# A three-layer interaction network with a row tower: layer 1's operand is written without its norm by ScalarE, and the norm is applied in two VectorE steps where layer 1 ends

## The chip, the cores and the metric

One core of a Trainium2 chip. The metric is the device time of one launch in microseconds (us). PE is TensorE, DVE is VectorE, ACT is ScalarE, POOL is GpSimd, SP is SyncE (it issues most transfers). Float32 throughout.

## The reference

For each of 512 samples, 39 fields pick one row of 16 numbers each from their tables; this is x (39 fields by 16 dimensions d). Three layers follow, each with 128 units:

```
prev = x                                     # 39 x 16, later 128 x 16
for k in 0, 1, 2:
    t[o, d] = sum over m, h of  W_k[m, h, o] * x[m, d] * prev[h, d]   + b_k[o]
    t = t / sqrt(sum over o and d of t*t)    # one norm per sample
    logit_k = t ; prev = t
z = sum over d of the three t's, concatenated        # 384 per sample
y = relu(relu([z, dense] @ W_top1 + b_top1) @ W_top2 + b_top2) @ W_top3
```

The norm is one number per sample. Layer 1 is linear in prev, so a norm left out of prev can be applied to layer 1's sum before the bias.

## The kernel before, in words

**Tiles.** 512 samples are 16 tiles of 32; a tile has 32 x 16 = 512 columns (sample, d), one PSUM bank wide. Units lie on the 128 partitions. Tiles 1 to 14 run in a hardware loop (`Fori`) on each engine, tiles 0 and 15 are written out before and behind it, with hand-written order in each and semaphores between them.

**A layer (k = 1 or 2) of a tile** is 11 chunks c0 to c10 of `xb`, the rows of x broadcast over the partitions by DMA. DVE writes the products z = `t_ps[k-1]` x `xb` (L651), PE multiplies them with the weights. Chunks c0, c2, c7, c10 are direct (2 or 3 fields, L820). The other seven hold four fields that are treated as two pairs in a scheme like Strassen's: POOL makes the sums `t2` (L354) and `t41` (L357) of the products (for c5 and c6 of layer 1 DVE and ACT make `t2`, L664 and L517), and PE takes 28 matmuls on products and sums (L834), the last ones after a wait on `t41`. z is a ring of 14 rows, so DVE waits for PE to free rows. Layer 0 works on `xr`, products of x with shifted x (L634), into `acc0` (L811).

**Order on PE** in a tile: layer 1 (c0 to c10), layer 0 of the next tile, layer 2 (c0 to c5), the small matmuls for the norms (`add_partitions`, L879), layer 2 (c6 to c10).

**Where layer 1 ends.** After c9 ACT copies parts of the pair sums (`carry`, L527 to L531), DVE adds them in five small steps into `v` (`shared_sums`, L672 to L683), then `add_shared` (L685): for k = 1 one scalar_tensor_tensor, raw12 = acc1 + bias + v (L691). ACT copies raw12 to `t_ps[1]` (L538), layer 2's operand, and squares it (L541). For k = 2 `add_shared` is already two steps: acc2 += v (L694), raw12 = acc2 x norm of layer 1 (L697), and ACT adds the bias (L546, L547).

**Where layer 0 ends.** ACT reads `acc0` twice: squares (L494) and the value with its bias into `traw0` (L495). DVE sums both over d (`norm_sums`, at c5 of layer 2). At c8 DVE makes 1/norm of all three layers (`normalize`), at c9 it writes the features and then `t_ps[0]` = (acc0 + bias) x norm (`scale0`, L741), layer 1's operand for the next tile. PE's next layer 0 waits for `traw0` and `scale0`.

**POOL** also issues the gathers of table rows (L317): ten per tile, seven of them after c9 of layer 1, one after c6 and two after c9 of layer 2, for the tile after next. Before tile 0 it issues the gathers of tiles 0 and 1. **SP** writes gathered rows to DRAM (`write_rows`, L290) and loads `xb` (L410), x (L277) and `xr` (L283). At the start its order is: `xr` of tile 0; wait until all of it has landed; `xb` c0 to c5; the rows of tile 1 (a wait for their gathers); `xb` c6 to c10; x and `xr` of tile 1.

**Before tile 0** PE does layer 0, then the norm's matmul; DVE runs sum_squares, sum_d, normalize, features and scale0 before its first product of layer 1.

Of the kernel before, what the change touches and what calls it, by code (L numbers as in the profile page):

```python
# [5 lines left out]
ALU = mybir.AluOpType  # L6
# [5 lines left out]
P = 128  # L12
# [7 lines left out]
N = TILE_B * EMB  # L20
# [111 lines left out]
def build(nc, ids_in, base_in, masks_in, table, xt, xq, dense_t, w0a, w0b, w1, w2, b0, b1, b2,  # L132
          wt1, bt1, wt2, bt2, wt3, out):
    ctx = ExitStack()
    with ctx:
# [25 lines left out]
        ones = sb("ones", [P, UNITS // 2])  # L161
        traw0 = sb("traw0", [P, N])
        raw12 = sb("raw12", [P, N])
# [20 lines left out]
        h1, h2 = z[:, 0:4, :], z[:, 4:6, :]  # L184
        y_sb = traw0[:, 0:P]

# [38 lines left out]
        v_step, v_used = sem("v_step"), sem("v_used")  # L225
        scaled_ready = sem("scaled_ready")
        t1_ready, t0_ready = sem("t1_ready"), sem("t0_ready")
        sq_ready = [sem(f"sq_ready{k}") for k in range(LAYERS)]
        raw_ready = [sem("raw_ready0"), None, sem("raw_ready2")]
        ssum_ready = [sem(f"ssum_ready{k}") for k in range(LAYERS)]  # L230
# [70 lines left out]
        def _(pool):  # L301
# [71 lines left out]
            gather(0, range(GROUPS))  # L373
            mix_rows(0)
            gather(1, range(GROUPS))
            tile(0)
# [6 lines left out]
        def _(sp):  # L383
# [81 lines left out]
            for j in range(TOP1 // P):  # L465
# [7 lines left out]
            sp.dma_start(out.rearrange("(g n) a -> g (n a)", n=P),  # L473
                         traw0[0:P:Y_AT, 0:P]).then_inc(y_written, 16)
            sp.wait_ge(y_written, 16)

        @block.scalar
        def _(act):
# [10 lines left out]
            def evacuate0(i):  # L489
                act.wait_ge(acc0_ready, i + 1)  # L490
                if not at_first(i):
                    act.wait_ge(t0_ready, i)
                    act.wait_ge(feat_ready, i)
                nc.scalar.activation(sq[:, 0, :], acc0[:, :], ACT.Square, bias=bias[:, 0:1]).then_inc(sq_ready[0], 1)  # L494
                nc.scalar.activation(traw0[:, :], acc0[:, :], ACT.Identity,  # L495
                                     bias=bias[:, 0:1]).then_inc(raw_ready[0], 1)

# [35 lines left out]
            def evacuate1(i, last=False):  # L533
                act.wait_ge(v_used, mix_no(i, 1) + 1)
                if not last:

                    act.wait_ge(z0_ready, len(LOADS0) * (i + 2))
                nc.scalar.copy(t_ps[1][:, :], raw12[:, :]).then_inc(t1_ready, 1)  # L538
                if not at_first(i):
                    act.wait_ge(ssum_ready[2], i)  # L540
                nc.scalar.activation(sq[:, 1, :], raw12[:, :], ACT.Square).then_inc(sq_ready[1], 1)  # L541

# [55 lines left out]
        def _(dve):  # L598
# [86 lines left out]
            def add_shared(i, k):  # L685
                n = mix_no(i, k)
                dve.wait_ge(z_used, chunks_to(i, k, NCH - 1))
                dve.wait_ge(v_step, 5 * n + 5)
                dve.wait_ge(p1_ready, n + 1)
                if k == 1:  # L690
                    nc.vector.scalar_tensor_tensor(raw12[:, :], acc[1][:, :], bias[:, 1:2], v[:, :],  # L691
                                                   ALU.add, ALU.add).then_inc(v_used, 1)
                else:
                    nc.vector.tensor_tensor(acc[2][:, :], acc[2][:, :], v[:, :], ALU.add).then_inc(v_used, 1)  # L694

                    dve.wait_ge(v_used, n + 1)
                    nc.vector.tensor_tensor(by_sample(raw12[:, :]), by_sample(acc[2][:, :]),  # L697
                                            over_d(rnorm[:, 1, :]), ALU.mult).then_inc(scaled_ready, 1)

# [5 lines left out]
            def sum_d(k, i, into=dsum):  # L705
                if k != 1:
                    dve.wait_ge(raw_ready[k], i + 1)
                nc.vector.tensor_reduce(into[:, k, :], by_sample((traw0 if k == 0 else raw12)[:, :]),
                                        axis=AX_X, op=ALU.add).then_inc(dsum_ready, 1)
# [29 lines left out]

            def scale0(i):  # L740
                nc.vector.scalar_tensor_tensor(by_sample(t_ps[0][:, :]), by_sample(acc0[:, :]), bias[:, 0:1],  # L741
                                               over_d(rnorm[:, 0, :]), ALU.add, ALU.mult).then_inc(t0_ready, 1)

            def tile(i, first=False, last=False):
                for c in range(NCH):
                    products(i, 1, c)
                    later_t2(i, 1, c)
                    if c == 1 and not first:
                        shared_sums(i - 1, 2)
                    if c == 3 and not first:  # L750
                        add_shared(i - 1, 2)
                    if c == 7 and not first:
                        norm_sums(2, i - 1)
                    if c == 9 and not last:
                        products0(i + 1, (0, 1, 2,))
                    if c == 10 and not last:
                        products0(i + 1, (3,))
                shared_sums(i, 1)
                add_shared(i, 1)
                for c in range(NCH):  # L760
                    products(i, 2, c)
                    later_t2(i, 2, c)
                    if c == 3:
                        norm_sums(1, i)
                    if c == 5 and not last:
                        norm_sums(0, i + 1)
# [16 lines left out]
            for part in range(2, 4):  # L783
                mixed_weights(2, part)
            sum_squares(0, 0)
            sum_d(0, 0, dsum_alone)
            normalize(0, 0, 1)
            features(0, 0, 1, dsum_alone)
            scale0(0)
            tile(0, first=True)  # L790
# [11 lines left out]
        def _(pe):  # L802
            def layer0(i):
                if not at_first(i):
                    pe.wait_ge(raw_ready[0], i)
                    pe.wait_ge(t0_ready, i)
                for g, (k0, k1) in enumerate(LOADS0):
# [45 lines left out]
            def layer(i, k, chunks, first=False):  # L853
                for c in chunks:
                    if c == 0 and not at_first(i):
                        if k == 1:
                            pe.wait_ge(v_used, mix_no(i - 1, 1) + 1)
                        else:
                            pe.wait_ge(scaled_ready, i)
# [24 lines left out]
            def tile(i, first=False, last=False):  # L884
                layer(i, 1, range(NCH), first)
                if not last:
# [7 lines left out]
            layer0(0)  # L894
            add_partitions(0, 0, 1)
            tile(0, first=True)
# [7 lines left out]
            pe.wait_ge(feat_ready, TILES + 1)  # L904
            pe.wait_ge(raw_ready[0], TILES)
            pe.wait_ge(v_used, mix_no(TILES - 1, 1) + 1)
            for j in range(TOP1 // P):
# [92 lines left out]
```

## Time and profile before

| | us |
|---|---|
| median of 3 runs | 1155.6 |
| lowest and highest | 1154.4, 1155.64 |
| the profiled execution's own time | 1153.28 |
| its span (first to last instruction) | 1151.4 |
| busy: PE | 1106.4 (96%) |
| busy: DVE | 989.2 (86%) |
| busy: POOL | 944.0 (82%) |
| busy: ACT | 144.1 (13%) |

Times in the rows are microseconds from the span's start. A busy time is the union of an engine's instructions. In a timeline a row gives start, duration, engine, line, operation, what it writes and reads, how many instructions were merged, and in brackets the engine's idle time before it with what ended it. L plus a number is a line of the kernel before.

### The profile page before, as it was taken

The page shows a single profiled execution, that of the slowest core. Times are in us where ns is not written, and L with a number is a line of the kernel's source. Part 1 is how long each engine was busy: PE and PEld are TensorE (multiplying, and loading weights), DVE is VectorE, ACT ScalarE, POOL GpSimd, SP SyncE. Part 2 cuts the span into 40 slices and gives each one's busy share as a digit, 9 for nine tenths or more (in the row PEclk, how much of TensorE's full clock was granted, in tenths as well). Part 3 has the DMA queues.
Part 4 walks back from the last instruction along what each step waited for, and adds up shares of the span by engine and source line. Part 5 has one row for each costly group of instructions (what it writes and reads, how often), then busy time and mean ns, then how long its engine had stood idle before and what let it go on. Part 6 is the DMA issues. An engine that isn't in the chain of part 4 may idle for free. (4 is left out here: it accounts for less than half of the span.)

```text
span 1151.4 us, 22377 instructions
## 1 busy us (share of the span) xinstructions
PE 1106.4 (96%) x8264; PEld 595.0 (52%) x8264; DVE 989.2 (86%) x875; ACT 144.1 (13%) x298; POOL 944.0 (82%) x646
## 2 busy tenths in 40 slices
PE   0799999999999999999999999999999999999998
PEld 0355555455555545555554555555455555545553
DVE  2789989898998989899898989989898998989782
ACT  0010111101011110101111010111101011110102
POOL 4679888897988889898888989889898988958680
PEclk9899999999999999999999999999999999999999
DMA  7869366372936637293672829366282845628010
GB/s 235 275 223 326 90 230 202 109 263 62 325 101 216 213 99 267 65 325 104 210 220 95 269 68 318 110 213 217 85 279 68 304 125 199 226 75 286 1 52 1
DMA packets 103183, 205.81 MB, mean 179 GB/s; under 512 B 49918, under 2 KB 56258, under 8 KB 103164
## 3 DMA queue, kind: packets, MB, share of 16 engines
q1 hardware_dynamic: 94474, 203.89, 52.6%
q0 software_dynamic: 5120, 1.29, 1.4%
q10 hardware_dynamic: 3570, 0.37, 0.3%
q8 instruction: 13, 0.21, 0.1%
q14 instruction: 6, 0.05, 0.0%
HBM read 203.05 MB, written 2.46 MB: 178 GB/s over the span
## 5 line engine op out<-in xcount | busy, mean ns | idle before, releaser
L651 DVE TENSOR_TENSOR z<-t_ps,xb 128x2048 f32<-128x2048 f32 (+2 forms) x352 | 708.2, 2041 | 62.0 <-PE acc L834 43.9
L357 POOL TENSOR_TENSOR sums<-z,sums 128x1024 f32<-128x1024 f32 x224 | 531.0, 2374 | 45.2 <-DVE sums L664 30.1
L820 PE MATMUL acc<-z,w_sb 128*64 128x512 f32 x1408 | 324.5, 597 | 8.2 <-DVE z L651 8.2
L834 PE MATMUL mix_ps<-sums,s_sb 128*64 128x256 f32 x1792 | 327.7, 379 | 0.6 <-POOL sums L357 0.5
L354 POOL TENSOR_TENSOR sums<-z 128x512 f32<-128x512 f32 x192 | 245.7, 1280 | 71.0 <-DVE z L651 68.1
L834 PE MATMUL mix_ps<-z,w_sb 128*64 128x256 f32 x896 | 267.4, 380 | 0.0
L834 PE MATMUL acc<-z,w_sb 128*64 128x256 f32 x896 | 267.4, 380 | 0.0
L834 PE MATMUL acc<-z,s_sb 128*64 128x256 f32 x896 | 266.7, 379 | 0.0
L834 PE MATMUL p_ps<-z,w_sb 128*64 128x256 f32 x896 | 266.7, 379 | 0.0
L834 PEld LDWEIGHTS mix_ps<-sums,s_sb 128*64 128x64 f32 x1792 | 185.6, 137 | 100.3 <-POOL sums L357 6.2
L834 PE MATMUL acc<-sums,w_sb 128*64 128x256 f32 x896 | 230.4, 380 | 0.0
L317 POOL DMA_INDIRECT gathered<-in_table,rows_of x160 | 153.8, 961 | 52.7 <-issue 36.5
L820 PEld LDWEIGHTS acc<-z,w_sb 128*64 128x64 f32 x1408 | 101.4, 138 | 169.3 <-issue 149.6
L834 PEld LDWEIGHTS acc<-z,w_sb 128*64 128x64 f32 x896 | 122.2, 137 | 104.6 <-issue 51.5
L834 PEld LDWEIGHTS acc<-z,s_sb 128*64 128x64 f32 x896 | 123.1, 137 | 64.9 <-issue 0.3
L811 PE MATMUL acc<-xr,w_sb 117*64 117x512 f32 x448 | 101.6, 605 | 31.9 <-DVE xr L634 31.9
L834 PEld LDWEIGHTS p_ps<-z,w_sb 128*64 128x64 f32 x896 | 123.1, 137 | 0.0
L834 PEld LDWEIGHTS mix_ps<-z,w_sb 128*64 128x64 f32 x896 | 122.1, 137 | 0.0
L834 PEld LDWEIGHTS acc<-sums,w_sb 128*64 128x64 f32 x896 | 121.1, 137 | 0.0
L811 PEld LDWEIGHTS acc<-xr,w_sb 117*64 117x64 f32 x448 | 32.8, 140 | 97.2 <-issue 96.4
L634 DVE TENSOR_TENSOR xr<-t_ps,xr 117x1024 f32<-117x1024 f32 (+1 forms) x60 | 62.6, 1082 | 2.3 <-DMA xr<-xt 2.3
L527 ACT COPY cross<-mix_ps 64x256 f32<-64x256 f32 x32 | 11.7, 364 | 394.3 <-PE acc L834 394.3
(80 smaller groups left out, 445.1 us busy)
## 6 DMA issues: line engine op xcount, KB each, us to landing
xb<-xt SPq DMA_DIRECT2D x128, 512.0 KB, 6.2
xb<-xq SPq DMA_DIRECT2D x112, 512.0 KB, 4.9
xb<-xt SPq DMA_DIRECT2D x48, 768.0 KB, 6.5
xr<-xt SPq DMA_DIRECT2D x48, 468.0 KB
w_sb<-in_w SPq DMA_DIRECT2D x2, 2496.0 KB, 16.5
xr<-xt SPq DMA_DIRECT2D x16, 234.0 KB
x<-xt SPq DMA_DIRECT2D x15, 234.0 KB
gathered<-in_table,rows_of POOLq DMA_INDIRECT x160, 2.9
```

The lines of the kernel that those rows point to most:

```text
L317: nc.gpsimd.indirect_dma_start(gathered[0:n, g, :], None, table[:, :], bass.IndirectOffsetOnAxis(rows_of[0:n, g:g + 1], 0)).then_inc(rows_ ...
L354: nc.gpsimd.tensor_tensor(t2, t3, b11, ALU.add).then_inc(pool_t2, 1)
L357: nc.gpsimd.tensor_tensor(t41, b2, t2_twice, ALU.subtract).then_inc(t41_ready, 1)
L527: nc.scalar.copy(cross[RIGHT, N2], mix_ps[LEFT, N2]).then_inc(cross_ready, 1)
L634: nc.vector.tensor_tensor(xr[:, k0:k1, :], x.rearrange("p (a n) -> p a n", a=1).broadcast_to([WIDE, k1 - k0, N]), xr[:, k0:k1, :], ALU.mul ...
L651: nc.vector.tensor_tensor(z[:, at:at + n, :], t_ps[k - 1][:, :].rearrange("p (a n) -> p a n", a=1).broadcast_to([P, n, N]), xb[:, XB_ROW[c ...
L811: last = nc.tensor.matmul(acc0[o, :], w0_sb[:, k, o], xr[:, k, :], start=(k == 0), stop=(k == STEPS0 - 1))
L820: last = nc.tensor.matmul(acc[k][o, :], w_sb[k][:, field + r, o], z[:, at + r, :], start=(c == 0 and r == 0), stop=(c == NCH - 1 and r == ...
L834: return nc.tensor.matmul(bank[side, cols], weights, moving, start=start, stop=stop, skip_group_check=True)
```

## The change

- `scale0` and `traw0` are gone. ACT writes acc0 + bias (no norm) to `t_ps[0]`, ahead of the square, once all of layer 1's products of the running tile exist. `t0_ready` is signalled there; the sum over d reads `t_ps[0]` instead of `traw0`. PE's next layer 0 waits for the square alone.
- Layer 1 now ends as layer 2 does: acc1 += v, then raw12 = acc1 x norm of layer 0, two DVE instructions for one. ACT adds the bias while it writes `t_ps[1]`, squares with the bias, and has a third instruction, raw12 = raw12 + bias, for the sum over d.
- In tile 0 the norm of layer 0 is no longer ahead of the first product: DVE does sum_squares and sum_d after c1, normalize and features after c2; PE does the norm's matmul after c1.
- POOL waits for the first `xr` load of tile 0 before it issues the gathers of tile 1.

```diff
@@ gpsimd
             gather(0, range(GROUPS))
             mix_rows(0)
+            pool.wait_ge(xr_loaded[0], 16)
             gather(1, range(GROUPS))
@@ scalar: evacuate0, evacuate1
                 act.wait_ge(acc0_ready, i + 1)
                 if not at_first(i):
-                    act.wait_ge(t0_ready, i)
-                    act.wait_ge(feat_ready, i)
+                    act.wait_ge(z_ready, STEPS * (i - 1) + NCH)
+                nc.scalar.activation(t_ps[0][:, :], acc0[:, :], ACT.Identity, bias=bias[:, 0:1]).then_inc(t0_ready, 1)
+                if not at_first(i):
+                    act.wait_ge(ssum_ready[0], i)
                 nc.scalar.activation(sq[:, 0, :], acc0[:, :], ACT.Square, bias=bias[:, 0:1]).then_inc(sq_ready[0], 1)
-                nc.scalar.activation(traw0[:, :], acc0[:, :], ACT.Identity,
-                                     bias=bias[:, 0:1]).then_inc(raw_ready[0], 1)
...
-                act.wait_ge(v_used, mix_no(i, 1) + 1)
                 if not last:
                     act.wait_ge(z0_ready, len(LOADS0) * (i + 2))
-                nc.scalar.copy(t_ps[1][:, :], raw12[:, :]).then_inc(t1_ready, 1)
+                act.wait_ge(scaled1_ready, i + 1)
+                nc.scalar.activation(t_ps[1][:, :], raw12[:, :], ACT.Identity, bias=bias[:, 1:2]).then_inc(t1_ready, 1)
                 if not at_first(i):
                     act.wait_ge(ssum_ready[2], i)
-                nc.scalar.activation(sq[:, 1, :], raw12[:, :], ACT.Square).then_inc(sq_ready[1], 1)
+                nc.scalar.activation(sq[:, 1, :], raw12[:, :], ACT.Square, bias=bias[:, 1:2]).then_inc(sq_ready[1], 1)
+                nc.scalar.activation(raw12[:, :], raw12[:, :], ACT.Identity, bias=bias[:, 1:2]).then_inc(raw_ready[1], 1)
@@ vector: add_shared, tile
-                if k == 1:
-                    nc.vector.scalar_tensor_tensor(raw12[:, :], acc[1][:, :], bias[:, 1:2], v[:, :],
-                                                   ALU.add, ALU.add).then_inc(v_used, 1)
-                else:
-                    nc.vector.tensor_tensor(acc[2][:, :], acc[2][:, :], v[:, :], ALU.add).then_inc(v_used, 1)
...
+                nc.vector.tensor_tensor(acc[k][:, :], acc[k][:, :], v[:, :], ALU.add).then_inc(v_used, 1)
+
+                dve.wait_ge(v_used, n + 1)
+                nc.vector.tensor_tensor(by_sample(raw12[:, :]), by_sample(acc[k][:, :]), over_d(rnorm[:, k - 1, :]),
+                                        ALU.mult).then_inc(scaled1_ready if k == 1 else scaled_ready, 1)
...
+                    if c == 1 and first:
+                        sum_squares(0, 0)
+                        sum_d(0, 0, dsum_alone)
+                    if c == 2 and first:
+                        normalize(0, 0, 1)
+                        features(0, 0, 1, dsum_alone)
...
-                        if not last:
-                            scale0(i + 1)
@@ tensor: layer0, tile
-                    pe.wait_ge(raw_ready[0], i)
-                    pe.wait_ge(t0_ready, i)
+                    pe.wait_ge(sq_ready[0], i)
...
+                if first:
+                    layer(i, 1, range(2), first)
+                    add_partitions(0, 0, 1)
+                    layer(i, 1, range(2, NCH))
+                else:
+                    layer(i, 1, range(NCH))
```

## Rows read from the trace of the kernel before

**Rows 1.** Windows: us, PE, PEld, DVE, ACT, POOL busy, granted clock, DMA share, GB/s.

```profile
79.00:1091.00 1012.00, 1012.00 (x7689) 548.00 (x7686) 911.54 (x794) 129.49 (x270) 868.88 (x583) 1.00 0.55 181
```

**Rows 2.** Waits of PE: us in total, times, longest.

```profile
PE acc L820 <- DVE z L651: 8.2, 3, 3.7
```

**Rows 3.** Groups by line and form: busy us, mean ns of one, idle before.

```profile
L691 DVE SCALAR_TENSOR_TENSOR raw<-acc,bias,v 128x512 f32<-128x512 f32 x16 | 12.0, 751 | 0.7
L741 DVE SCALAR_TENSOR_TENSOR t_ps<-acc,bias,rnorm 128x512 f32<-128x512 f32 x16 | 12.0, 749 | 0.0
...
L547 ACT ACTIVATE raw<-raw,bias 128x512 f32<-128x512 f32 x16 | 11.3, 706 | 0.0
L697 DVE TENSOR_TENSOR raw<-acc,rnorm 128x512 f32<-128x512 f32 x16 | 11.1, 691 | 0.6
...
L694 DVE TENSOR_TENSOR acc<-acc,v 128x512 f32<-128x512 f32 x16 | 10.9, 682 | 0.1
...
L538 ACT COPY t_ps<-raw 128x512 f32<-128x512 f32 x16 | 9.4, 589 | 24.1 <-DVE raw L691 24.1
```

**Rows 4.** Timeline of DVE where layer 1 ends, a middle tile.

```profile
620.48 0.75 DVE L691 SCALAR_TENSOR_TENSOR raw<-acc,bias,v 128x512 f32<-128x512 f32 x1
622.05 7.28 DVE L651 TENSOR_TENSOR z<-t_ps,xb 128x1024 f32<-128x1024 f32 x4 [0.82 <-ACT t_ps L538]
```

**Rows 5.** Timeline of POOL, same tile: last gather, layer 2's c1, c3 and c6.

```profile
624.74 0.94 POOL L317 DMA_INDIRECT gathered<-in_table,rows_of  x1 [0.30 <-issue]
625.70 1.28 POOL L354 TENSOR_TENSOR sums<-z 128x512 f32<-128x512 f32 x1
627.06 2.37 POOL L357 TENSOR_TENSOR sums<-z,sums 128x1024 f32<-128x1024 f32 x1
629.42 1.27 POOL L354 TENSOR_TENSOR sums<-z 128x512 f32<-128x512 f32 x1
...
642.01 2.37 POOL L357 TENSOR_TENSOR sums<-z,sums 128x1024 f32<-128x1024 f32 x1
```

**Rows 6.** Timeline of PE: first matmul behind `t41`, chunks c1 and c6.

```profile
629.84 0.38 PE L834 MATMUL acc<-sums,w_sb 128*64 128x256 f32 x1
...
644.66 0.38 PE L834 MATMUL acc<-sums,w_sb 128*64 128x256 f32 x1
```

**Rows 7.** Last tile: timelines where layer 1 ends; the chain's step before c6.

```profile
1093.49 7.29 DVE L651 TENSOR_TENSOR z<-t_ps,xb 128x1024 f32<-128x1024 f32 x4 [0.66 <-ACT t_ps L538]
...
1097.06 1.27 POOL L354 TENSOR_TENSOR sums<-z 128x512 f32<-128x512 f32 x1 [9.10 <-DVE z L651]
...
1116.41 0.04 issue
```

**Rows 8.** Timelines of ACT, DVE and PE before and in tile 0.

```profile
40.78 0.69 ACT L494 ACTIVATE sq<-acc,bias 128x512 f32<-128x512 f32 x1 [37.16 <-PE acc L811]
...
44.86 7.28 DVE L651 TENSOR_TENSOR z<-t_ps,xb 128x1024 f32<-128x1024 f32 x4
...
75.41 1.23 DVE L634 TENSOR_TENSOR xr<-t_ps,xr 117x1024 f32<-117x1024 f32 x1 [1.49 <-DMA xr<-xt]
...
78.36 2.80 PE L820 MATMUL acc<-z,w_sb 128*64 128x512 f32 x12 [1.52 <-DVE z L651]
```

**Rows 9.** Timelines at the start: gathers of tile 1, first `xr`, SP's issues.

```profile
26.59 1.00 POOL L317 DMA_INDIRECT gathered<-in_table,rows_of  x1 [0.81 <-POOL rows_of L311]
...
30.48 1.23 DVE L634 TENSOR_TENSOR xr<-x,xr 117x1024 f32<-117x1024 f32 x1 [4.56 <-DMA xr<-xt]
...
36.15 0.37 SPq L410 DMA_DIRECT2D xb<-xt  x1
...
43.92 8.41 SPq L290 DMA_DIRECT2D xt<-gathered  x3
```

**Rows 10.** Windows at the start, columns as in Rows 1.

```profile
42.00:52.00 10.00, 6.08 (x28) 2.88 (x30) 9.74 (x12) 0.23 (x2) 3.56 (x2) 0.66 1.02 401
...
58.00:74.00 16.00, 16.00 (x139) 10.12 (x136) 12.73 (x9) 1.77 (x3) 13.20 (x7) 1.00 0.95 357
```

More of the change, by code:

```diff
@@ L161, in build @@
         ones = sb("ones", [P, UNITS // 2])
-        traw0 = sb("traw0", [P, N])
         raw12 = sb("raw12", [P, N])
@@ L184, in build @@
         h1, h2 = z[:, 0:4, :], z[:, 4:6, :]
-        y_sb = traw0[:, 0:P]
+        y_sb = v[:, 0:P]
         acc0 = pb("acc0")
@@ L225, in build @@
         v_step, v_used = sem("v_step"), sem("v_used")
-        scaled_ready = sem("scaled_ready")
+        scaled1_ready, scaled_ready = sem("scaled1_ready"), sem("scaled_ready")
         t1_ready, t0_ready = sem("t1_ready"), sem("t0_ready")
         sq_ready = [sem(f"sq_ready{k}") for k in range(LAYERS)]
-        raw_ready = [sem("raw_ready0"), None, sem("raw_ready2")]
+        raw_ready = [t0_ready, sem("raw_ready1"), sem("raw_ready2")]
         ssum_ready = [sem(f"ssum_ready{k}") for k in range(LAYERS)]
@@ L473, in _ @@
             sp.dma_start(out.rearrange("(g n) a -> g (n a)", n=P),
-                         traw0[0:P:Y_AT, 0:P]).then_inc(y_written, 16)
+                         v[0:P:Y_AT, 0:P]).then_inc(y_written, 16)
             sp.wait_ge(y_written, 16)
@@ L689, in add_shared @@
                 dve.wait_ge(p1_ready, n + 1)
-                if k == 1:
-                    nc.vector.scalar_tensor_tensor(raw12[:, :], acc[1][:, :], bias[:, 1:2], v[:, :],
-                                                   ALU.add, ALU.add).then_inc(v_used, 1)
-                else:
-                    nc.vector.tensor_tensor(acc[2][:, :], acc[2][:, :], v[:, :], ALU.add).then_inc(v_used, 1)
-                    dve.wait_ge(v_used, n + 1)
-                    nc.vector.tensor_tensor(by_sample(raw12[:, :]), by_sample(acc[2][:, :]),
-                                            over_d(rnorm[:, 1, :]), ALU.mult).then_inc(scaled_ready, 1)
+                nc.vector.tensor_tensor(acc[k][:, :], acc[k][:, :], v[:, :], ALU.add).then_inc(v_used, 1)
+                dve.wait_ge(v_used, n + 1)
+                nc.vector.tensor_tensor(by_sample(raw12[:, :]), by_sample(acc[k][:, :]), over_d(rnorm[:, k - 1, :]),
+                                        ALU.mult).then_inc(scaled1_ready if k == 1 else scaled_ready, 1)
             def sum_squares(k, i):
@@ L705, in sum_d @@
             def sum_d(k, i, into=dsum):
-                if k != 1:
-                    dve.wait_ge(raw_ready[k], i + 1)
-                nc.vector.tensor_reduce(into[:, k, :], by_sample((traw0 if k == 0 else raw12)[:, :]),
+                dve.wait_ge(raw_ready[k], i + 1)
+                nc.vector.tensor_reduce(into[:, k, :], by_sample((t_ps[0] if k == 0 else raw12)[:, :]),
                                         axis=AX_X, op=ALU.add).then_inc(dsum_ready, 1)
@@ L738, in features @@
                                         ALU.mult).then_inc(feat_ready, 1)
-            def scale0(i):
-                nc.vector.scalar_tensor_tensor(by_sample(t_ps[0][:, :]), by_sample(acc0[:, :]), bias[:, 0:1],
-                                               over_d(rnorm[:, 0, :]), ALU.add, ALU.mult).then_inc(t0_ready, 1)
             def tile(i, first=False, last=False):
@@ L784, in _ @@
                 mixed_weights(2, part)
[L785 to L789, printed above, removed]
             tile(0, first=True)
@@ L856, in layer @@
                         if k == 1:
-                            pe.wait_ge(v_used, mix_no(i - 1, 1) + 1)
+                            pe.wait_ge(scaled1_ready, i)
                         else:
@@ L884, in tile @@
             def tile(i, first=False, last=False):
-                layer(i, 1, range(NCH), first)
+                if first:
[4 more added lines that the diff above has]
+                    layer(i, 1, range(NCH))
                 if not last:
@@ L894, in _ @@
             layer0(0)
-            add_partitions(0, 0, 1)
             tile(0, first=True)
@@ L904, in _ @@
             pe.wait_ge(feat_ready, TILES + 1)
-            pe.wait_ge(raw_ready[0], TILES)
-            pe.wait_ge(v_used, mix_no(TILES - 1, 1) + 1)
+            pe.wait_ge(sq_ready[0], TILES)
+            pe.wait_ge(scaled1_ready, TILES)
             for j in range(TOP1 // P):
```

## The prediction

> **What bounds the kernel now.** I read the windows first, because they show at once whether an engine has any time to give. From 79 to 1091 us, the whole run but its two ends, PE is busy 1012.00 of 1012.00 us at full granted clock [rows 1]. The list of waits agrees: in the whole run PE waited for products only 3 times, 8.2 us in all [rows 2]: before the first product, before c10 of tile 0, and where layer 1 of the last tile ends. The change leaves PE's work as it is. So fifteen of the sixteen tiles can't become shorter, whatever DVE or ACT save; they can only become longer, if something makes PE wait. A gain can come from the start or the end alone.
>
> The question is then how close the others run behind PE, and busy shares don't tell it. I took the timelines of DVE, POOL and PE around the place where layer 1 ends in one middle tile. PE covers this place with c10, layer 0 of the next tile and c0 of layer 2. Behind this cover runs the chain that the change lengthens: DVE's last step on layer 1, ACT's write of the operand, DVE's products of c0 and c1, POOL's sums for c1, PE. It ends close: POOL's second sum ends at 627.06 + 2.37 = 629.43 [rows 5], and PE's first matmul on the far side of it starts at 629.84 [rows 6]. The spare is 0.41 us, less 0.04 us that the signal takes [rows 7]: 0.37 us. For c6 it is 644.66 - (642.01 + 2.37) = 0.28 us.
>
> **The change, part by part.**
>
> *Layer 1's end.* One DVE instruction of 0.751 us becomes two of 0.682 and 0.691, which layer 2's end already has [rows 3]: +0.62 us. The new pair sits exactly where DVE is the only engine working on the chain. ACT's plain copy into `t_ps[1]` takes 0.589; the new form (Identity with bias, into PSUM) is not in the trace. Below it is the copy's 0.589, above it the Identity with bias into SBUF, 0.706 [rows 3]. I take 0.65, +0.06, for it is like both in one thing. The chain to layer 2's first product gets 0.68 us longer (0.62 to 0.74).
>
> On the price of ACT the Trainium skill has a figure: ScalarE: Activation LUTs, Rules for kernel authors, budgets about 0.3 us plus 0.83 ns per element, an estimate of 0.725 us for 512 elements. By it the chain would be 0.76 us longer and the forecast 0.9 us higher; the copy's row at 0.589 lies below that budget, so I stay with the rows.
>
> *What reaches PE.* In the last tile, where POOL was idle, it started 1097.06 - 1093.49 = 3.57 us after DVE's first product [rows 7]. In the middle tile that rule gives 622.05 + 3.57 = 625.62 [rows 4]; POOL started at 625.70, just behind its last gather (624.74 + 0.94) [rows 5], so 0.08 us is hidden by the gather. POOL then starts 0.68 - 0.08 = 0.60 later, and PE must wait 0.60 - 0.37 = 0.23 us. It does so in each of tiles 1 to 14, for the next tile's chain starts again from PE: 14 x 0.23 = 3.2 us. With the ends of the chain's price it is 14 x 0.17 = 2.4 and 14 x 0.29 = 4.1. POOL goes on without a pause (629.42 follows 629.43) [rows 5], so the delay also reaches c6 with its spare of 0.28 - 0.04 + 0.23 = 0.47: up to 0.13 us more per tile, 1.8 in all, if POOL never catches up. I take none of it, because POOL stands behind a product and not behind itself at one step between; it goes into the range. In tile 0 POOL has no gather there and PE comes to layer 2 after its own wait; I take nothing.
>
> *Last tile.* There is no next layer 0 to cover the end of layer 1, and the chain of waits runs through this very place. The whole 0.68 is paid: +0.7.
>
> *`scale0` gone.* 16 x 0.749 = 12 us of DVE work [rows 3]. It stood at c9 of layer 2, covered by PE, which never waited there. Worth 0; DVE will wait longer for PE.
>
> *ACT.* Its third instruction (0.7 us) comes behind the write that DVE waits for, and ACT, busy 129 of 1012 us [rows 1], has nothing queued behind it but the evacuation of layer 0, which waits for PE. Worth 0. The same goes for the new order of `t_ps[0]` and square, for the reduce that now reads PSUM, and for the waits on `z_ready` and `ssum_ready`, long past when ACT comes to them.
>
> *The start.* Before, ACT's square begins at 40.78 and the first product at 44.86 [rows 8]. Now ACT writes the operand first: 40.78 + 0.69 = 41.47, and DVE can begin 3.4 us earlier. I cost this at nothing, because the next thing that is late is a transfer. PE's c10 of tile 0 starts at 78.36 after a wait, behind products that waited for `xr` of tile 1 until 75.41 [rows 8]: 75.41 + 1.23 + 1.7 (c10's product of three fields, an estimate from thirteen fields in 7.28 us) = 78.3. From there on PE never waits, so this transfer sets the clock for the rest. The transfers before it run at full share: 1.02 and 0.95 of 16 engines at 401 and 357 GB/s [rows 10]. The earlier DVE doesn't start one of them earlier.
>
> *POOL's new wait.* `xr`'s first part landed at 30.48 [rows 9], so POOL's gathers of tile 1, which began at 26.59, 0.81 us behind their address step, begin some 1.2 us after 30.48 (an estimate: those 0.81 and the step itself), 5 us later. For it: the rest of `xr` and then `xb` (from 36.15) may come earlier, by at most the 1.5 us that I allow. Against it: SP's writes of tile 1's rows wait for these gathers; they came at 43.92 and took until 52.33, most of it with full queues [rows 9], and would now come near 49. That still fits before 52.33 if the queues have drained, and costs up to 1.5 if not; SP's loads of c6 to c10 are queued behind. I take 0, with -1.5 and +1.5 as ends. The norm work now between c1 and c3 of tile 0 makes DVE wait for PE and ACT some 2 us in a stretch where DVE later waits for transfers anyway.
>
> Sum: 3.2 + 0.7 + 0 = +3.9 us. The profiled execution took 1153.28, which gives 1157.2; the median of the three runs stands 2.3 above that execution, so the forecast is 1155.6 + 3.9 = **1159.5 us**. Its own range is 1155.6 + (2.4 + 0.7 - 1.5) = 1157.2 to 1155.6 + (4.1 + 1.8 + 0.8 + 1.5) = 1163.8.
>
> **The rivals.**
>
> *A. The shorter start reaches the end.* If the `xr` loads of tile 1 can come earlier with the rest, 3.4 us are won there and +3.9 paid elsewhere: 1156.1, no change. For it: POOL's new wait leaves the first loads alone. Against it: the full share of the transfer engines [rows 10].
>
> *B. The start was bound by compute: faster.* Place: 41 to 78 us. PE's granted clock was 0.66 on average from 42 to 52, half rate (1.2 GHz) for most of it, behind the gap before the first product [rows 10]. If the gap shrinks and the clock stays at 2.4 GHz, PE's 6.08 busy us there would take 4.0 by the mean clock, or 3.1 if nearly all of them ran at half rate; I take 3.0 us won, and with 3.4 for the earlier start 6.4 are won: 1155.6 + 3.9 - 6.4 = 1153.1. It decides only if `xr` of tile 1 lands before about 72 instead of 75.4. The Trainium skill, TensorE: Matmul & The Clock Gate, Rules for kernel authors, advises against idle gaps between bursts of matmuls since they bring the clock down. The drop in this trace agrees; that PE was the late one there is what the wait at 78.36 speaks against.
>
> *C. The cover holds.* If ACT's and DVE's hand-overs take 0.2 us less than I count, the 14 waits vanish: +0.7, 1156.3, the same. The 0.62 of DVE alone exceed 0.37 + 0.08, which speaks against it. With A it would be 1155.6 + 0.7 - 3.4 = 1152.9, faster.
>
> *D. The late gathers cost.* SP stands 2 us or more longer before the loads of c6: 1161.5 or above.
>
> *E. A rule on fusing.* The Trainium skill, VectorE: DVE Perf Modes, Rules for kernel authors, says that the number of DVE instructions counts, not their semaphores. By instructions alone the change is even (one more at layer 1's end, `scale0` gone), and the time would be that of before but for the start, case A's side. The rows say that place decides, and the two places differ: one is covered, one is not.
>
> **How the numbers follow.** Forecast 0.50, D 0.10, A with E's reading 0.13, C 0.10, B 0.10, A and C together 0.07. A change of 0.2%, 2.3 us, is about what a measurement of this kernel can tell. Slower: forecast and D, 0.60. Same: A and C, 0.23. Faster: B and A with C, 0.17. The range of 8 in 10 is 1152.8 to 1162.5: it takes in the faster cases at its low end and leaves out the top of D and of the forecast's own range.
>
> **What the profile will show.** If right: two DVE rows of 0.68 and 0.69 at layer 1's end and 2.2 us instead of 1.57 to the first product behind them; a POOL start near 626.3 in a tile like this one; about 14 small gaps of 0.2 us in PE before `acc<-sums` of c1, layer 2; PE's wait before c10 of tile 0 growing from 1.5 or staying, with its start still near 78.4; DVE less busy by 16 x (0.749 - 0.62) = 2 us. Wrong would be: PE without gaps between tiles, or c10 of tile 0 well before 77.

## The result, and the profile after

| | before | after |
|---|---|---|
| median | 1154.4 (7 runs) | 1160.5 (7 runs) |
| lowest and highest | 1153.2, 1155.6 | 1158.6, 1163.1 |
| profiled execution, span | 1153.3, 1151.4 | 1160.5, 1158.7 |

The change makes the kernel slower: the ratio is 1.005, with a 95% interval of 1.0032 to 1.0069, that is 3.7 to 8.0 us. The medians differ by 6.1 us; 3.9 were forecast. The two profiled executions differ by more, 7.2 us in their spans.

Line numbers of after differ: the products are L655, the two steps of a layer's end L694 and L697, ACT's operand L541, POOL's sums L353 and L356, PE's pair matmuls L827.

PE is no longer busy throughout. The windows of after, with the columns of [rows 1]; the row there was 1012.00 of 1012.00:

```profile
80.00:1098.00 1018.00, 1017.35 (x7692) 545.49 (x7688) 911.63 (x796) 141.83 (x286) 869.01 (x583) 1.00 0.55 180
```

The 0.65 us are only the idle time that exceeds PE's pipeline, which the profile models as busy. The honest measure is the distance between equal instructions. The timelines of PE give the first matmul behind `t41` of c1 in layer 2, for tile 0 and tile 14, in before:

```profile
90.88 0.38 PE L834 MATMUL acc<-sums,w_sb 128*64 128x256 f32 x1
...
1034.16 0.38 PE L834 MATMUL acc<-sums,w_sb 128*64 128x256 f32 x1
```

and in after:

```profile
92.26 0.43 PE L827 MATMUL acc<-sums,w_sb 128*64 128x256 f32 x1
...
1040.48 0.43 PE L827 MATMUL acc<-sums,w_sb 128*64 128x256 f32 x1
```

In before that is 943.28 / 14 = 67.38 us a tile, in after 948.22 / 14 = 67.73: 0.35 us more in each of 14 tiles, 4.9 us. From tile 14 to tile 15 the same distance grew from 66.68 to 67.58, 0.9 us for the last tile. Its matmuls, in before and in after:

```profile
1100.84 0.43 PE L834 MATMUL acc<-sums,w_sb 128*64 128x256 f32 x1
...
1108.06 0.43 PE L827 MATMUL acc<-sums,w_sb 128*64 128x256 f32 x1
```

The tail behind it takes 50.6 us in both. The rest of the spans' difference, 1.4 us, lies ahead of tile 0's layer 2.

The place where layer 1 ends, in the tile that answers to [rows 4], timeline of DVE in after:

```profile
624.50 0.70 DVE L694 TENSOR_TENSOR acc<-acc,v 128x512 f32<-128x512 f32 x1
625.23 0.69 DVE L697 TENSOR_TENSOR raw<-acc,rnorm 128x512 f32<-128x512 f32 x1
626.77 7.28 DVE L655 TENSOR_TENSOR z<-t_ps,xb 128x1024 f32<-128x1024 f32 x4 [0.85 <-ACT t_ps L541]
```

From the start of the last step to the first product it is 2.27 us, against 1.57: the chain is 0.70 longer. POOL and PE behind it, to set beside [rows 5] and [rows 6]:

```profile
628.76 0.94 POOL L316 DMA_INDIRECT gathered<-in_table,rows_of  x1 [0.30 <-issue]
630.27 1.29 POOL L353 TENSOR_TENSOR sums<-z 128x512 f32<-128x512 f32 x1 [0.57 <-issue]
631.64 2.38 POOL L356 TENSOR_TENSOR sums<-z,sums 128x1024 f32<-128x1024 f32 x1
634.13 1.27 POOL L353 TENSOR_TENSOR sums<-z 128x512 f32<-128x512 f32 x1
...
646.53 2.37 POOL L356 TENSOR_TENSOR sums<-z,sums 128x1024 f32<-128x1024 f32 x1
```

```profile
634.08 0.43 PE L827 MATMUL acc<-sums,w_sb 128*64 128x256 f32 x1
...
648.97 0.43 PE L827 MATMUL acc<-sums,w_sb 128*64 128x256 f32 x1
```

The gather no longer touches the first sum: POOL stands idle 0.57 us before it. POOL's `t41` of c1 ends at 634.02 and PE starts 0.06 later, where 0.41 lay between them before. At c6 it is the same: 648.90 and 648.97, where 0.28 lay before. The chain sets PE's time at two places of each tile.

How much falls at each place is read from PE's matmuls around the wait. Timeline of PE at c1, before and then after:

```profile
629.40 0.81 PE L834 MATMUL mix_ps<-sums,s_sb 128*64 128x256 f32 x5
629.84 0.38 PE L834 MATMUL acc<-sums,w_sb 128*64 128x256 f32 x1
630.04 0.38 PE L834 MATMUL mix_ps<-sums,s_sb 128*64 128x256 f32 x1
...
633.41 1.09 PE L827 MATMUL mix_ps<-sums,s_sb 128*64 128x256 f32 x5
634.08 0.43 PE L827 MATMUL acc<-sums,w_sb 128*64 128x256 f32 x1
634.34 0.38 PE L827 MATMUL mix_ps<-sums,s_sb 128*64 128x256 f32 x1
```

From the first of these rows to the third it is 0.64 us in before and 0.93 in after. Over tiles 1 to 14 the mean growth is 0.27 us at c1: 0.22 of waiting, and 0.05 because the matmul behind a wait takes 0.43 us instead of 0.38 and the next starts that much later. At c6 the mean is 0.03 of waiting and the same 0.05. Together that is the 0.35.

ACT's write and the two DVE steps, groups by line and form in after (busy, mean ns of one, idle before; the DVE groups hold the ends of layers 1 and 2):

```profile
L697 DVE TENSOR_TENSOR raw<-acc,rnorm 128x512 f32<-128x512 f32 x32 | 22.1, 691 | 1.1
L694 DVE TENSOR_TENSOR acc<-acc,v 128x512 f32<-128x512 f32 x32 | 22.1, 691 | 0.8
...
L541 ACT ACTIVATE t_ps<-raw,bias 128x512 f32<-128x512 f32 x16 | 11.1, 691 | 33.8 <-issue 27.5 <-DVE raw L697 6.3
```

The start, from the timelines of ACT, DVE and PE in after, to set beside [rows 8]:

```profile
39.98 0.66 ACT L496 ACTIVATE t_ps<-acc,bias 128x512 f32<-128x512 f32 x1 [36.35 <-PE acc L804]
...
40.67 1.22 DVE L655 TENSOR_TENSOR z<-t_ps,xb 128x1024 f32<-128x1024 f32 x1 [0.99 <-ACT t_ps L496]
43.79 2.29 DVE L655 TENSOR_TENSOR z<-t_ps,xb 128x2048 f32<-128x2048 f32 x1 [1.89 <-DMA xb<-xt]
...
51.36 0.36 DVE L717 RECIPROCAL inv<-nrm_ps 128x32 f32<-128x32 f32 x1 [2.42 <-ACT nrm_ps L556]
...
76.80 1.22 DVE L638 TENSOR_TENSOR xr<-t_ps,xr 117x1024 f32<-117x1024 f32 x1 [1.27 <-DMA xr<-xt]
...
79.74 2.79 PE L813 MATMUL acc<-z,w_sb 128*64 128x512 f32 x12 [1.50 <-DVE z L655]
```

DVE's first product starts 4.2 us earlier: 3.4 by the change, and 0.8 because layer 0 ended that much earlier in this execution (ACT's first instruction begins at 39.98, against 40.78). Nothing of it is left. The second product waits for its load (1.89 us), the norm that now stands inside the tile costs a wait of 2.42, and PE's c10 comes 1.4 us later than before, behind the same transfer.

PE's granted clock is 1.00 in the stretch where it was 0.66 before [rows 10], and that wins nothing either. Windows of after, columns as in [rows 1]:

```profile
42.00:52.00 10.00, 6.39 (x46) 3.10 (x48) 5.72 (x7) 0.18 (x1) 7.12 (x8) 1.00 1.02 389
```

### The profile page after: what moved, and what is told of

Same layout as the page of the kernel before. It is cut to its first block and busy times, and to the rows that moved or that the text cites. A ratio compares the mean times of both kernels' runs of the same rounds, so it can differ in the third digit from the quotient of the medians.

```text
span 1158.7 us, 22379 instructions
## 1 busy us (share of the span) xinstructions
PE 1108.5 (96%) x8264; PEld 590.0 (51%) x8264; DVE 988.3 (85%) x875; ACT 156.8 (14%) x314; POOL 944.1 (81%) x646
## 5 line engine op out<-in xcount | busy, mean ns | idle before, releaser
L655 DVE TENSOR_TENSOR z<-t_ps,xb 128x2048 f32<-128x2048 f32 (+2 forms) x352 | 708.4, 2041 | 58.2 <-PE acc L827 37.1
L356 POOL TENSOR_TENSOR sums<-z,sums 128x1024 f32<-128x1024 f32 x224 | 531.0, 2374 | 44.5 <-DVE sums L668 29.4
L827 PE MATMUL mix_ps<-sums,s_sb 128*64 128x256 f32 x1792 | 332.8, 380 | 4.5 <-POOL sums L356 3.7
L353 POOL TENSOR_TENSOR sums<-z 128x512 f32<-128x512 f32 x192 | 245.7, 1280 | 73.7 <-DVE z L655 65.8
L827 PE MATMUL acc<-z,w_sb 128*64 128x256 f32 x896 | 267.4, 380 | 3.4 <-issue 2.2
L827 PE MATMUL mix_ps<-z,w_sb 128*64 128x256 f32 x896 | 267.3, 380 | 0.0
L827 PE MATMUL acc<-z,s_sb 128*64 128x256 f32 x896 | 267.0, 380 | 0.0
L827 PE MATMUL p_ps<-z,w_sb 128*64 128x256 f32 x896 | 267.0, 380 | 0.0
L827 PEld LDWEIGHTS mix_ps<-sums,s_sb 128*64 128x64 f32 x1792 | 182.5, 137 | 112.7 <-POOL sums L356 25.2
L827 PE MATMUL acc<-sums,w_sb 128*64 128x256 f32 x896 | 232.0, 381 | 0.0
L827 PEld LDWEIGHTS acc<-z,w_sb 128*64 128x64 f32 x896 | 121.9, 137 | 108.1 <-issue 57.3
L827 PEld LDWEIGHTS acc<-z,s_sb 128*64 128x64 f32 x896 | 123.0, 137 | 64.9
L827 PEld LDWEIGHTS p_ps<-z,w_sb 128*64 128x64 f32 x896 | 123.0, 137 | 0.0
L827 PEld LDWEIGHTS mix_ps<-z,w_sb 128*64 128x64 f32 x896 | 121.9, 137 | 0.0
L827 PEld LDWEIGHTS acc<-sums,w_sb 128*64 128x64 f32 x896 | 118.1, 137 | 0.0
```

What stands on the lines that cost most here:

```text
L353: nc.gpsimd.tensor_tensor(t2, t3, b11, ALU.add).then_inc(pool_t2, 1)
L356: nc.gpsimd.tensor_tensor(t41, b2, t2_twice, ALU.subtract).then_inc(t41_ready, 1)
L655: nc.vector.tensor_tensor(z[:, at:at + n, :], t_ps[k - 1][:, :].rearrange("p (a n) -> p a n", a=1).broadcast_to([P, n, N]), xb[:, XB_ROW[c ...
L827: return nc.tensor.matmul(bank[side, cols], weights, moving, start=start, stop=stop, skip_group_check=True)
```

## The experiments

The theory after the result: the loss is the 0.70 us on the chain at layer 1's end, less a cover, in each of tiles 1 to 14, and in full in the last tile; the start gives and takes nothing that outlasts the spread of runs. The rivals: the late gathers cost the 1.4 us at the start; or something else in the change costs (the sum over d that now reads PSUM, ACT's third instruction, the new order on ACT).

**e1: the changed kernel without POOL's wait.**

```diff
             mix_rows(0)
-            pool.wait_ge(xr_loaded[0], 16)
             gather(1, range(GROUPS))
```

> The changed kernel without POOL's wait for the first xr load. Theory (the cost of the start is the late gathers of tile 1): c10 of tile 0 starts near 78.4 us instead of 79.7, the period of a middle tile stays 67.73 us, the time is 1.3 us below the changed kernel, some 5.5 us above the kernel before. Rival (the start is late for another cause, the norm's chain that now stands inside tile 0): c10 stays near 79.7 and the time with it. Rival A (a shorter start reaches the end once the wait is gone): c10 near 75.

Measured: median 1160.2 us, ratio to before 1.0049 (1.0032 to 1.0065), the changed kernel's own within 0.3 us. Gathers of tile 1 begin at 26.59 again; c10 of tile 0 starts at 78.86, the period is 67.73. The wait isn't the loss. The expected 1.3 us did not come: c10 moved 0.9 in the profile, and the time less than the runs spread.

**e2: before, with layer 1's end in two steps and nothing else** (the new semaphore's declaration is left out here).

```diff
...
-                    nc.vector.scalar_tensor_tensor(raw12[:, :], acc[1][:, :], bias[:, 1:2], v[:, :],
-                                                   ALU.add, ALU.add).then_inc(v_used, 1)
+                    nc.vector.scalar_tensor_tensor(acc[1][:, :], acc[1][:, :], bias[:, 1:2], v[:, :],
+                                                   ALU.add, ALU.add).then_inc(split_step, 1)
+                    dve.wait_ge(split_step, i + 1)
+                    nc.vector.tensor_tensor(by_sample(raw12[:, :]), by_sample(acc[1][:, :]),
+                                            over_d(ones[:, 0:TILE_B]), ALU.mult).then_inc(v_used, 1)
```

> The kernel before with one thing added: layer 1's end is two DVE instructions (0.75 and 0.69 us; the second multiplies by one), so the chain there is 0.72 us longer, as in the changed kernel (0.70); scale0, the start and ACT stay. Theory (the length of this chain alone makes the steady loss): the period goes from 67.39 to 67.73 to 67.76 us, PE waits behind POOL's sums at c1 and c6 of layer 2 in each of tiles 1 to 14, the start is that of before (c10 of tile 0 at 78.4), the last tile pays 0.72; the time is 5 to 6 us above before. Rival (the loss comes from something else of the change: PSUM reads, ACT's third instruction, the order on ACT): period 67.39, only 0.7 us lost.

Measured: 1160.8 us, ratio 1.0051 (1.0034 to 1.0068): this one edit makes the whole loss. Timeline of DVE, then of PE for tiles 0 and 14:

```profile
622.17 0.76 DVE L692 SCALAR_TENSOR_TENSOR acc<-acc,bias,v 128x512 f32<-128x512 f32 x1
622.97 0.69 DVE L695 TENSOR_TENSOR raw<-acc,ones 128x512 f32<-128x512 f32 x1
624.48 1.23 DVE L652 TENSOR_TENSOR z<-t_ps,xb 128x1024 f32<-128x1024 f32 x1 [0.82 <-ACT t_ps L539]
```

```profile
89.83 0.38 PE L838 MATMUL acc<-sums,w_sb 128*64 128x256 f32 x1
...
1038.45 0.43 PE L838 MATMUL acc<-sums,w_sb 128*64 128x256 f32 x1
```

From L692 to the product 2.31 us, 0.74 more than before; the period is 67.76, inside what was expected. In the last tile 67.55 stands for 66.68. The sum over d from PSUM, ACT's third instruction and the order on ACT are not in this kernel, so that rival falls.

**e3 and e4: small DVE instructions in the same place, as a dose.** 64 columns each, two (e3, shown) and four of them (e4, `range(4)`), into a part of `cross` that nobody uses:

```diff
+                    for r in range(2):
+                        spare = cross[LEFT, H + r * UNITS // 2:H + (r + 1) * UNITS // 2]
+                        nc.vector.tensor_tensor(spare, ones[LEFT, :], ones[LEFT, :], ALU.add)
                     nc.vector.scalar_tensor_tensor(raw12[:, :], acc[1][:, :], bias[:, 1:2], v[:, :],
```

> The kernel before with two small DVE instructions (64 columns, about 0.2 us each) ahead of layer 1's last step, some 0.4 us in all. Theory (a cover of 0.37 at PE and 0.08 at POOL must be used up first): no wait of PE at c1, period 67.39 to 67.43 us (c6 may lose some hundredths, its spare being 0.24 and the delay there 0.32), last tile +0.4; the time 0.4 to 1 us above before, no measurable change. Rival (every 0.1 us on this chain costs 0.05 us per tile at once, without a cover): period 67.6, 3 us.

> The same with four such instructions, some 0.85 us. Theory (beyond the cover the loss grows one for one): period 67.39 + (0.85 - 0.36) = 67.88 us, 14 x 0.49 + 0.85 = 7.7 us above before. Rival (the loss saturates since POOL catches up): 5 to 6 us as with 0.7.

The dose came out smaller than expected. The instructions overlap; timelines of DVE of e3 and e4:

```profile
623.21 0.35 DVE L693 TENSOR_TENSOR cross<-ones 64x64 f32<-64x64 f32 x2
623.48 0.74 DVE L694 SCALAR_TENSOR_TENSOR raw<-acc,bias,v 128x512 f32<-128x512 f32 x1
```

```profile
621.66 0.62 DVE L693 TENSOR_TENSOR cross<-ones 64x64 f32<-64x64 f32 x4
622.21 0.74 DVE L694 SCALAR_TENSOR_TENSOR raw<-acc,bias,v 128x512 f32<-128x512 f32 x1
```

From the first to L694 it is 0.27 and 0.55 us. e3 took 1155.2 us, ratio 1.0000 (0.9987 to 1.0014); e4 1156.6, ratio 1.0026 (1.0013 to 1.0039). The periods, each from the two PE rows as above (e3 93.59 and 1036.87, e4 90.75 and 1036.64):

| kernel | longer chain, us | period, us | loss per tile |
|---|---|---|---|
| before | 0 | 67.38 | 0 |
| e3 | 0.27 | 67.38 | 0.00 |
| e4 | 0.55 | 67.56 | 0.19 |
| after | 0.70 | 67.73 | 0.35 |
| e2 | 0.74 | 67.76 | 0.38 |

Nothing at 0.27, and at the three points from 0.55 on the loss is the length less 0.36. That is a cover, not a slope from zero; no run lies between 0.27 and 0.55. By place the picture is finer. The share of c1, read as above, is 0.11, 0.27 and 0.31 us in e4, after and e2, while c6 takes 0.08 to 0.09 in all three: once PE waits at c1, that wait covers c6 too. In e3, where PE waits at neither, the spare left is 0.22 at c1 and 0.14 at c6 (means of tiles 1 to 14), so c6 is the first to be used up. The 7.7 us that were expected of e4 fall with the dose: by its period 14 x 0.19 + 0.55 = 3.2 us would be due, and 3.0 (1.5 to 4.5) were measured. The expected saturation (5 to 6 us) is not seen either.

**e5: e2 with one of POOL's sums between c1 and c6 of layer 2 given to DVE and ACT.**

```diff
-T2_LATER = {(1, 5): 0, (1, 6): 1}
+T2_LATER = {(1, 5): 0, (1, 6): 1, (2, 4): 0}
```

> The kernel of e2 (before, with layer 1's end in two steps) with one of POOL's sums between c1 and c6 of layer 2 (t2 of c4, 1.28 us) moved to DVE and ACT. It asks where the loss of 0.37 us per tile sits. Theory (c1 takes what exceeds some 0.49 us of delay, about 0.23, and c6 the rest, since POOL runs without a pause from c1 to c6): c6's wait goes, c1's stays, the period falls from 67.76 to 67.6. Rival (c1 takes all): 67.76 as before. Rival (POOL as a whole is too slow): the period falls to 67.4. The added DVE and ACT work (0.7 and 0.6 us) lies behind products and should cost nothing.

Measured: 1158.0 us, ratio 1.0036 (1.0023 to 1.0050), period 67.68. c6's wait is gone (POOL ends 0.22 us ahead of PE there), c1's has stayed. So of e2's 0.38 us some 0.30 fall at c1 and 0.08 at c6. The expected 67.6 was 0.08 too low. Neither rival fits: c1 doesn't take all, and POOL as a whole isn't too slow.

**e6 to e8: can the earlier start be kept?** e6 is before with the rows of tile 1 written from ACT's queue, e7 the same in the changed kernel without POOL's wait:

```diff
             for c in range(NCH):
                 load_chunk(0, c)
-                if c == NCH // 2:
-                    write_rows(sp, 1)
@@ scalar (e6; in e7 the new line stands ahead of square_root)
             square_root(0, 0, 1)
+            write_rows(act, 1)
             tile(0, first=True)
```

> The kernel before, but the rows of tile 1 are written from ACT's queue, so SP issues the loads of c6 to c10 of tile 0 right behind those of c5. Theory (c10 of tile 0 and all behind it is set by the stream of loads): c6 lands earlier, x and xr of tile 1 by up to 2 us, and c10 of tile 0 starts at 76.7 to 77.5 us, where PE's own backlog begins to set it; 1 to 1.5 us below before, hardly measurable. Rival (the writes' many small packets are the cost, wherever they are issued): no change, 78.4.

> The changed kernel without POOL's wait and with the rows of tile 1 written from ACT's queue. Theory (the shorter start can only reach the end if the loads come earlier too): c10 of tile 0 at 76 to 77.5 us against 78.9 in e1; period 67.73; 1.5 to 3 us below the changed kernel. Rival (the norm's chain inside tile 0 has become the bound): c10 stays at 78.5 to 79.

Neither expectation came true, nor did their rivals fully. e6 took 1155.6 us, ratio 1.0013 (1.0001 to 1.0024), c10 at 78.93; e7 1161.4, ratio 1.0068 (1.0054 to 1.0081), c10 at 80.60. SP's issues in e6:

```profile
46.49 2.20 SPq L410 DMA_DIRECT2D xb<-xt  x2
65.71 0.84 SPq L277 DMA_DIRECT2D x<-xt  x1
66.60 4.42 SPq L283 DMA_DIRECT2D xr<-xt  x4
```

The loads up to c10 are issued by 48.7, but x and `xr` of tile 1 only from 65.7. They read what the writes put into DRAM, and the last of the writes, issued at 45.68, now lands at 65.69, behind the last of the loads (65.28). The view of the tensor `xt` up to there (loads and writes together) says up to 20.0 us from issue to landing; the 20.0 is that write's:

```profile
DMA to landing us min/median/max: 6.7/16.1/20.0
```

From 58 to 74 us the transfer engines are then busy for 0.71 of the time, against 0.95 in [rows 10]. What sets the start is not the volume of the loads alone, but gathers, writes and loads one after the other.

e8 takes tile 0 from the changed kernel (operand without norm, two steps at its end) and all other tiles from before, ACT's writes as in e7, and one more edit in the last tile:

```diff
-                        if k == 2 and c == PADS_AT and last:
+                        if k == 2 and c == 6 and last:
                             nc.gpsimd.memset(xb[:, 3:5, :], 0.0).then_inc(pads_ready, 1)
```

> Tile 0 as in the changed kernel (operand without norm, two steps at layer 1's end), all other tiles as before; rows of tile 1 from ACT's queue; POOL's memset in the last tile moved from c3 to behind c6 of layer 2, for it stands in the chain of the last tile (0.95 us). Theory (the loss is in the repeated two-step end, the possible gain in the start and the last tile): period 67.39, c10 of tile 0 at 76 to 77.5, the last tile 0.9 us shorter; 1.5 to 3 us below before, near 1152. Rival: the start does not move, 0.9 us below before.

Measured: 1154.3 us, ratio 1.0006 (0.9998 to 1.0015), so the expected gain did not come. The period is 67.39 (PE rows at 92.39 and 1035.88): with the two steps in tile 0 alone the steady loss is gone. The tail is 0.7 us shorter (49.9 for 50.6), the memset's part. But c10 of tile 0 comes at 79.9: ACT stands in its writes while DVE waits for the norm, 5.36 us in the timeline of DVE:

```profile
53.15 0.36 DVE L735 RECIPROCAL inv<-nrm_ps 128x32 f32<-128x32 f32 x1 [5.36 <-ACT nrm_ps L558]
```

**e9 and e10: c10's product ahead of tile 1's layer 0 products, in tile 0**, and e8's memset edit; e9 on before, e10 on the changed kernel without POOL's wait:

```diff
-                    if c == 9 and not last:
+                    if c == 9 and not (first or last):
                         products0(i + 1, (0, 1, 2,))
                     if c == 10 and not last:
-                        products0(i + 1, (3,))
+                        products0(i + 1, (0, 1, 2, 3) if first else (3,))
```

> The kernel before with two edits at its ends: in tile 0 DVE makes the product of c10 ahead of the products of layer 0 of tile 1 (whose xr lands last), and in the last tile POOL's memset stands behind c6 of layer 2. Theory (the start is late because c10 stands behind transfers it doesn't need; the last tile because 0.95 us of memset is in POOL's chain): PE starts c10 of tile 0 when its backlog allows, near 76.7, layer 0 of tile 1 near 79.3 instead of 81.0, a gain of 1 to 1.7 us; the last tile 0.7 us shorter (as in e8); period 67.39; together 2 us below before. Rival (layer 0 of tile 1 then waits for its last xr): only the 0.7 us.

> The changed kernel without POOL's wait and with the two edits of e9. Theory: the steady part stays (period 67.73), start and last tile gain what e9 gains, 1.5 to 2.4 us; 1158 to 1159, still 4 us above before. Rival (in the changed kernel PE's backlog in tile 0 is itself later because DVE waits for the norm): c10 gains less than 1 us.

e9: 1153.4 us, ratio 0.9996 (0.9987 to 1.0005). e10: 1160.8, ratio 1.0065 (1.0051 to 1.0079). In both PE's wait before c10 is gone. It came back later: in e9 PE waits at c1 of layer 2 of tile 0, in e10 in three places around it. PE's rows with idle time in e9:

```profile
47.09 3.68 PE L820 MATMUL acc<-z,w_sb 128*64 128x512 f32 x8 [3.68 <-DVE z L651]
92.27 0.43 PE L834 MATMUL mix_ps<-sums,s_sb 128*64 128x256 f32 x1 [1.38 <-POOL sums L357]
```

The reason is in the timeline of DVE in e9:

```profile
75.40 1.76 DVE L651 TENSOR_TENSOR z<-t_ps,xb 128x1536 f32<-128x1536 f32 x1 [3.31 <-PE acc L834]
77.08 4.08 DVE L634 TENSOR_TENSOR xr<-t_ps,xr 117x1024 f32<-117x1024 f32 x4
81.18 0.42 DVE L672 TENSOR_TENSOR cross<-cross,mix_ps 64x256 f32<-64x256 f32 x1
```

c10's product has to wait for PE to free rows of z, 3.31 us, the time in which DVE made three of tile 1's four layer 0 products before. Now all four stand behind it, and the small sums of layer 1's end begin at 81.18 instead of 78.93. e10 shows the same wait, 3.31. e9's median is 0.8 us below that of before in the same comparison, and not told apart from it.

e10 was expected at 1158 to 1159 and lies near e1 instead, so even the memset's 0.7 us did not show. In its profile the tail is 49.7 us, but the last tile takes 68.49 for after's 67.58. There PE's granted clock is 0.50 to 0.52 from 1102 to 1108, behind the wait where layer 1 ends. The matmuls of c1 take about 0.6 us there instead of 0.38, and POOL's first sum for c4 then waits 0.59 us for DVE, and DVE's product for it 0.84 for PE. In after the low clock is over sooner, ahead of the wait for POOL's sum, which covers it. Windows, the first of e10 and the second of after:

```profile
1106.00:1108.00 2.00, 2.00 (x14) 1.19 (x12) 2.00 (x2) 0.00 (x0) 1.86 (x1) 0.52 0.99 363
...
1106.00:1108.00 2.00, 1.88 (x14) 1.10 (x10) 2.00 (x2) 0.00 (x0) 2.00 (x2) 0.82 0.88 332
```

That the clock cost e10 the 0.7 us is argued from this one profile and not shown by a run of its own; how it stands in e10's other executions is open.

**e11: before with POOL's wait alone** (the line of e1, added).

> The kernel before with POOL's new wait alone. Theory (the start of this kernel varies from run to run by more than the wait costs): median within 1 us of before; gathers of tile 1 begin near 31.6, SP's writes near 48.5, the loads of c6 near 53, c10 of tile 0 between 77.5 and 80. Rival: the late gathers cost 1.4 us, as the first profile of the changed kernel suggests.

Measured: 1153.4 us, ratio 0.9998 (0.9986 to 1.0009). SP's writes begin at 47.70 and c10 starts at 78.31. The wait costs nothing that can be measured in time, so the 1.4 us at the start of the changed kernel's profile are not its price.

c10's start alone hides something. In e11's profile PE's wait before c10 is 2.70 us, and behind it the granted clock falls:

```profile
78.31 4.14 PE L821 MATMUL acc<-z,w_sb 128*64 128x512 f32 x12 [2.70 <-DVE z L652]
...
80.00:82.00 2.00, 2.00 (x6) 0.48 (x4) 1.07 (x3) 0.58 (x2) 1.70 (x2) 0.50 0.13 8
```

c10's twelve matmuls take 4.14 us against 2.80 [rows 8]. e3 (a wait of 3.38) and e6 (3.50) show the same fall to about half; in the other profiles the clock stays at 1.00 from 76 to 84 us. From c10 to layer 0 it then takes 3.9 to 4.3 us instead of 2.6.

The starts of e2, e3 and e4, which are before's to the instruction up to c10 of tile 0, put that matmul at 77.3, 79.7 and 78.2, and the matmul of c1 in layer 2 at 89.8, 93.6 and 90.8. A difference of 1.4 us between two profiles at that place shows nothing.

## Why the prediction was right

The forecast was slower, 1159.5 us with an own range of 1157.2 to 1163.8; 1160.5 was measured. Point by point:

- *PE is saturated, so the middle can only lose.* Shown: in the middle window DVE is busy 912 us before and after, `scale0`'s 12 us are gone and replaced, and no tile is shorter.
- *The chain's price.* Forecast 0.68, measured 0.70 in after. The two parts were each off by 0.03 to 0.05 and made up for it: from the start of layer 1's last steps to ACT's start (621.35 in before, 625.96 in after) it is 0.59 longer, for 0.62 forecast; from there to the product it is 0.11 longer, for 0.06. ACT's write takes 0.691 us, not 0.65; it lies between the two rows taken as bounds, near the upper one. The Trainium skill's budget (ScalarE: Activation LUTs, Rules for kernel authors), an estimate of 0.725, was the nearer figure for the write, by little. What the prediction says it would add to the forecast, 0.9 us, is 15 x 0.075 = 1.1 by its own terms.
- *The cover.* Forecast 0.08 by the gather and 0.37 at c1, together 0.45; for c1 alone e5 has 0.74 - 0.30 = 0.44. The sum is right, its parts partly by luck. Without a gather in its way POOL starts 3.51 us after the first product in a middle tile, not 3.57, so the gather hid more (0.14 in the mean of tiles 1 to 14). The signal from POOL to PE takes 0.06 where PE waits for it, not 0.04, so PE's spare was less (0.34 in the mean). The wait at c1 came out at 0.22, against 0.23; that a wait costs 0.05 more at the next matmul was in no term.
- *c6.* The step that was mis-sized: "I take none of it". The runs show 0.08 us per tile there (e5 against e2, and the matmuls of after). The reason that I gave, POOL standing behind a product, holds at one step and turns against it at another: c3's product has no gather before it to hide behind and comes the full 0.70 late, to 626.77 + 7.28 = 634.05, and POOL starts c3 at 634.13, 0.11 after it had ended c1. POOL gets some 0.15 us back at c4, where it waited for a product in before. In all it needs 18.63 us from the start of c1's sums to the end of c6's, against 18.68: it does not catch up. From 0.23 forecast to 0.35 measured per tile, 3.2 to 4.9 us in all: 0.08 of the 0.12 are c6, the rest the slower matmul behind the wait at c1. The own range held it, by the term of 1.8 us.
- *The last tile.* Forecast 0.68, measured 0.9 between two equal matmuls: 0.14 of it comes up in tile 14, behind c1, and 0.76 is the longer chain in the last tile.
- *The start.* Forecast 0 with ends of 1.5. In time it is 0: e1 and e11 move nothing. The reason, a transfer sets c10, is what the profile of after shows again. That the transfers are bound by their engines' share alone was too simple; e6 shows the order gathers, writes, loads behind it.
- *Rival A and B* (the start reaches the end): refuted, c10 is no earlier in any run of the changed kernel but e10 (77.2, where the order was changed, and there the gain is spent by c1 of layer 2). B's condition on the clock did come true, 1.00 for 0.66 from 42 to 52 us, and won nothing, as c10 waited for a transfer. B cites the Trainium skill (TensorE: Matmul & The Clock Gate; the advice against idle gaps stands there under Why this matters for your kernels). The profiles of e3, e6 and e11 agree, with the clock at about half behind PE's waits of 2.7 to 3.5 us before c10; no median shows a price for it. *C* (the cover holds): refuted by the period. *D* (late gathers): refuted by e11. *E* (the Trainium skill, VectorE: DVE Perf Modes, Rules for kernel authors: the number of instructions counts): the counts of DVE instructions are equal, 875 and 875, and the time is not; e3 has 32 more than before and costs nothing that can be measured, e2 has 16 more and costs 5.9 us by the ratio. In this kernel the place decides.

The sum of the measured terms is 14 x 0.35 + 0.9 = 5.8 us, against 6.1 between the medians and 5.8 by the ratio.

## What to carry to other kernels

Where one engine is busy all the time, work on another is free or costs one for one, and a cover decides which: measure it as the distance between the end of the last helper's instruction and the start of the bound engine's, less the signal's own time (0.06 us here), at every place behind the edit and not only the first. Fewer or cheaper instructions in a covered place don't pay for one more on the chain between two stages. Before work is put into an earlier start, follow what is late next to its root; here it was a write to DRAM that a later load reads.

## What the runs showed of the hardware

- DVE instructions with no wait between them overlap: 64 columns show 0.21 us each, but four of them and the gap to the next take 0.55 us from the first start, 0.14 each (e4). At 512 columns two reduces of 0.69 and 0.68 us in before start 0.59 apart (629.26 and 629.85). Where the second waits for the first, as at the end of a layer, it is 0.73 from start to start for 0.70.
- ACT's Identity with bias over 512 columns took 0.66 us from PSUM to PSUM, 0.69 from SBUF to PSUM and 0.71 from SBUF to SBUF; the copy from SBUF to PSUM 0.59.
- A PE matmul of 256 columns that had to wait for POOL started 0.06 us after POOL's end and took 0.43 us instead of 0.38 (after, c1 and c6 of tiles 1 to 14).
- PE's granted clock fell to about half behind waits of 2.70, 3.38 and 3.50 us before c10 (e11, e3, e6); c10's matmuls then took 4.14 us instead of 2.80 (e11).
- A transfer of many small pieces that is issued behind big ones from another queue isn't ahead of them: ACT's writes landed 16.6 to 20.0 us after their issue (e6). SP's issue of the same writes, in line with the loads, cost SP 8.4 us of issue time [rows 9]; they landed 4.7 to 10.1 us after it, and x of tile 1 was issued at 58.03 instead of 65.71.
